# Local attention in a six-layer Trainium2 kernel: turned keys stored block-diagonally, one score matmul for two heads, all scores of a step in one PSUM bank

## The reference, cut to what matters

```python
q = l2norm(q) * qs;  k = l2norm(k) * ksc            # then rotated by position
bk2, bv2 = look(bk), look(bv)                        # each window sees the one before it and itself
sim = jnp.einsum('bhwie,bhwje->bhwij', bq, bk2) * QK_SCALE
sim = jnp.where(mask, -jnp.finfo(sim.dtype).max, sim)
attn = jax.nn.softmax(sim, -1)                       # over 64 keys
out = jnp.einsum('bhwij,bhwje->bhwie', attn, bv2)
```

## Time and profile before

| quantity | value |
|---|---|
| median of three runs | 4539.4 us (4538.72 to 4546.72) |
| profiled execution | 4539.03 us |
| its span | 4537.2 us |
| mean granted TensorE clock | 0.962 |
| TensorE busy | 4247.6 us (94%) |
| VectorE busy | 3486.7 us (77%) |
| GpSimd busy | 2585.0 us (57%) |
| ScalarE busy | 2474.6 us (55%) |
| score matmuls, L1063 | 382.4 us busy, 24576 records, mean 219 ns |
| probabilities times values, L1090 | 425.3 us busy, 10752 records, mean 280 ns |
| mask, maximum, centring (L1148, L1152, L1158) | 268.7 + 265.5 + 290.2 us busy |
| copy of the turned keys, L1204 | 227.7 us busy, 384 of 593 ns |

### The profile page before, as it was taken

How to read it: one execution, slowest core, us unless ns; L and a number is a source line. 1 busy time by engine, 2 the same in 40 slices (tenths; PEclk the granted TensorE clock), 3 DMA queues, 4 the chain that set the end, 5 groups by cost and what they waited for, 6 DMA issues and landing times. The chain is left out here.

```text
span 4537.2 us, 151497 instructions
## 1 busy us (share of the span) xinstructions
PE 4247.6 (94%) x60907; PEld 2648.5 (58%) x60907; DVE 3486.7 (77%) x6001; ACT 2474.6 (55%) x5618; POOL 2585.0 (57%) x2727
## 2 busy tenths in 40 slices
PE   6999969799998999989999989999899998999998
PEld 5999848555553555544555535555355554455553
DVE  4776556599993899966999749999479996599984
ACT  4555521466663566644666536666356664366662
POOL 2222213477771777744777617777167775277770
PEclk9999989899998999989999999999899998999998
DMA  1000000000000000000000000000000000000001
GB/s 67 0 0 0 0 0 0 6 1 0 0 0 19 6 0 0 0 19 6 0 0 0 19 5 1 0 0 0 19 6 0 0 0 19 6 0 0 0 0 38
DMA packets 12332, 27.20 MB, mean 6 GB/s; under 512 B 2460, under 2 KB 6728, under 8 KB 11344
## 3 DMA queue, kind: packets, MB, share of 16 engines
q1 hardware_dynamic: 12240, 25.80, 1.6%
HBM read 23.69 MB, written 2.10 MB: 6 GB/s over the span
## 5 line engine op out<-in xcount | busy, mean ns | idle before, releaser
L954 POOL TENSOR_TENSOR w_t<-w_t 128x512 f32<-128x512 f32 x768 | 980.9, 1278 | 352.0 <-DVE w_t L1113 349.8
L1113 DVE TENSOR_TENSOR w_t<-banks,w_tab 128x512 f32<-128x512 f32 x1536 | 982.6, 682 | 32.4 <-PE banks L1023 10.8
L983 POOL TENSOR_TENSOR w_t<-w_t,w_rn 128x512 f32<-128x512 f32 x768 | 784.4, 1042 | 243.7 <-ACT w_rn L1217 243.7
L1010 PE MATMUL banks<-w_vo,w_xs 128*32 128x256 f32 x12288 | 823.6, 386 | 8.1 <-ACT w_us L1178 8.1
L1023 PE MATMUL banks<-w_qk,w_xs 128*128 128x512 f32 x1536 | 768.9, 623 | 0.0
L1010 PEld LDWEIGHTS banks<-w_vo,w_xs 128*32 128x32 f32 x12288 | 320.9, 109 | 501.9 <-issue 357.8
L1187 ACT ACTIVATE w_pr<-w_pr 128x512 f32<-128x512 f32 x384 | 241.9, 630 | 598.8 <-DVE w_pr L1158 598.8
L1178 ACT ACTIVATE w_us<-banks 128x512 f32<-128x512 f32 x768 | 457.4, 596 | 172.4 <-PE banks L1010 172.3
L1140 DVE TENSOR_REDUCE w_ss<-w_sq 128x16 f32<-128x1024 f32 x384 | 465.2, 1211 | 0.0
L1090 PE MATMUL banks<-w_us,w_prT 128*32 128x128 f32 x10752 | 425.3, 280 | 18.5 <-ACT w_prT L1211 5.9
L975 POOL TENSOR_TENSOR w_pr<-w_pr,w_rl 128x512 f32<-128x512 f32 x384 | 403.1, 1050 | 46.1 <-DVE w_rl L1128 46.1
(11 more groups left out here) (163 smaller groups left out, 6862.4 us busy)
## 6 DMA issues: line engine op xcount, KB each, us to landing
w_qk<-w_qk_in SPq DMA_DIRECT2D x7, 1024.0 KB, 4.8
w_v<-w_v_in SPq DMA_DIRECT2D x7, 512.0 KB, 5.6
w_o<-w_o_in SPq DMA_DIRECT2D x7, 512.0 KB, 6.4
m_w<-m_w_in SPq DMA_DIRECT2D x6, 342.0 KB
xT<-x_in SPq DMA_DIRECT2D x4, 512.0 KB
out<-kept SPq DMA_DIRECT2D x8, 256.0 KB, 2.4
m_w<-m_w_in SPq DMA_DIRECT2D x6, 171.0 KB
r_tab<-r_tab_in SPq DMA_DIRECT2D x1, 512.0 KB
```

Source lines behind the costliest of these rows:

```text
L954: nc.gpsimd.tensor_tensor(v1, v1, v2[:, :, ::-1, :], ALU.add).then_inc(S["added"], 1)
L983: nc.gpsimd.tensor_tensor(v1, v1, rn[j % 2][:, i * HALF:(i + 1) * HALF].unsqueeze(2) .broadcast_to([P, HALF, WD]), ALU.mult).then_inc(S["n ...
L1010: last = nc.tensor.matmul(banks[WIN * g:WIN * (g + 1), 2, lo:lo + 2 * P], x[:, WIN * w:WIN * (w + 1)], wvo[:, first:first + 2, :].rearrang ...
L1113: nc.vector.tensor_tensor(dst[j % 2][:, i * C:(i + 1) * C].rearrange("p (h d) -> p h d", d=WD), src, tab[:, 2 * t + cs, i * WD:(i + 1) * W ...
```

## The change

- `kT` gets a dimension of two and lives for the whole program (`w_kT`, 128 partitions x 8 pairs x 2 x 288). In slot `par` only the 64 partitions of that parity hold keys; the other 64 stay zero. VectorE sets the whole tile to zero once, in the first block of the program (4608 elements a partition). The zeroing by GpSimd in each layer, with its semaphore, is gone.
- The copy of the turned keys is two copies of 64 partitions, one for each slot. Both count `k_turned`, so TensorE waits for twice the count.
- The scores of a step are 16 matmuls with 128 rows, 32 columns of queries and 128 columns of keys: both slots, each with its two windows. Since the rows of the other head are zeros, one matmul gives the scores of two heads. All 512 columns of a step go to bank 5, in the order window half, parity, group, key.
- Mask and maximum read bank 5. The centring is one instruction of 512 elements, in the place of two of 256, so `centred` counts once a step.

The diff, cut to its core:

```diff
@@ program
+    w_kT = sb("w_kT", [P, WH // 2, 2, WIN + T])
...
+            nc.vector.memset(w_kT[:], 0.0)
@@ window_attention
-    kT = sb("w_kT", [P, WH // 2, WIN + T])
...
         def _(pool):
-            nc.gpsimd.memset(kT[:, :, 0:WIN], 0.0).then_inc(S["ready"], 1)
-            pool.wait_ge(S["ready"], passed(layer + 1))
-            pool.sem_inc(sem("gate"), 1)
...
                 if live(1):
                     pe.wait_ge(S["q_turned"], passed(n(1)))
-                    pe.wait_ge(S["k_turned"], passed(n(1)))
+                    pe.wait_ge(S["k_turned"], passed(n(1) * 2))
                     if live(2):
-                        pe.wait_ge(S["centred"], passed(n(2) * 2))
+                        pe.wait_ge(S["centred"], passed(n(2)))
                     pe.sem_inc(sem("gate"), 1)
                     tk, hk = j1 // 2, j1 % 2
-                    for par in range(2):
-                        rows = slice(64 * par, 64 * par + 64)
-                        bank = banks[:, 5 + par, 0:2 * P].rearrange("p (a g r) -> p g a r", a=2, r=WIN)
-                        for g in range(NPAIR):
-                            for w in range(NWIN):
-                                lo = tk * P + WIN * w
-                                last = nc.tensor.matmul(
-                                    bank[WIN * w:WIN * (w + 1), g],
-                                    qT[j1 % 2][rows, g, WIN * w:WIN * (w + 1)],
-                                    kT[rows, hk * NPAIR + g, lo:lo + 2 * WIN].rearrange("p (a r) -> p a r", r=WIN),
-                                    start=True, stop=True)
+                    score = banks[:, 5, :].rearrange("p (a b g r) -> p g a b r", a=2, b=2, r=WIN)
+                    for g in range(NPAIR):
+                        for w in range(NWIN):
+                            lo = tk * P + WIN * w
+                            keys = kT[:, hk * NPAIR + g, :, lo:lo + 2 * WIN].rearrange("p b (a r) -> p a b r", r=WIN)
+                            last = nc.tensor.matmul(score[WIN * w:WIN * (w + 1), g],
+                                                    qT[j1 % 2][:, g, WIN * w:WIN * (w + 1)], keys,
+                                                    start=True, stop=True)
                     last.then_inc(S["scored"], 1)
...
-                    for par in range(2):
-                        nc.vector.tensor_tensor(
-                            pr[j1 % 2][:, :, par * NPAIR:(par + 1) * NPAIR].rearrange("p a g r -> p g a r"),
-                            heads[:, par], mx[j1 % 2][:, par * NPAIR:(par + 1) * NPAIR].unsqueeze(2).unsqueeze(3)
-                            .broadcast_to([P, NPAIR, 2, WIN]), ALU.subtract).then_inc(S["centred"], 1)
+                    nc.vector.tensor_tensor(pr[j1 % 2][:], heads, mx[j1 % 2][:].unsqueeze(1).unsqueeze(3)
+                                            .broadcast_to([P, 2, HALF, WIN]), ALU.subtract).then_inc(S["centred"], 1)
...
-                    nc.scalar.activation(kT[:, hk * NPAIR:(hk + 1) * NPAIR, lo:lo + P],
-                                         banks[:, 4, :].rearrange("p (g k) -> p g k", k=P), ACT.Copy)\
-                        .then_inc(S["k_turned"], 1)
+                    for par in range(2):
+                        rows = slice(64 * par, 64 * par + 64)
+                        nc.scalar.activation(kT[rows, hk * NPAIR:(hk + 1) * NPAIR, par, lo:lo + P],
+                                             banks[rows, 4, :].rearrange("p (g k) -> p g k", k=P), ACT.Copy)\
+                            .then_inc(S["k_turned"], 1)
```

More of the change, by code:

```diff
@@ L61 @@
 w_centred w_exped w_totalled w_inverse w_weighted w_p_turned w_p_taken w_valued w_y_taken w_y_turned w_residual
-w_ready w_tabled
+w_tabled
 m_up m_gelued m_made m_down m_residual
@@ L864, in window_attention @@
 @scoped
-def window_attention(nc, sem, sb, layer, h, xT, spare0, spare1, banks, ident, wqk, wv, wo, base, scl, tab, mask,
+def window_attention(nc, sem, sb, layer, h, xT, spare0, spare1, banks, ident, wqk, wv, wo, base, scl, tab, mask, kT,
                      m_w1, m_w2, m_col):
@@ L891, in window_attention @@
         "guarded logged rnorm added normed turned q_turned k_turned u_made u_taken edged scored masked maxed centred "
-        "exped totalled inverse weighted p_turned p_taken valued y_taken y_turned residual ready tabled").split()}
+        "exped totalled inverse weighted p_turned p_taken valued y_taken y_turned residual tabled").split()}
     C = HALF * WD
@@ L1184, in iteration @@
                 if live(2):
-                    act.wait_ge(S["centred"], passed(n(2) * 2))
+                    act.wait_ge(S["centred"], passed(n(2)))
                     p = pr[j2 % 2][:].rearrange("p a h r -> p (a h r)")
```

12 lines of the change are left out of this document (6 added, 6 removed).

## The result

The changed kernel takes 4571.67 us (median of four runs, 4564.28 to 4575.9); the kernel before takes 4540.41 us beside it (4538.72 to 4546.72). The ratio is 1.0065, with an interval of 1.0047 to 1.0082: 0.65% slower, where I had forecast no change, and above my range. The profiled execution took 4575.9 us, its span 4574.1. Of rival A nothing came true.

A forecast was written before the change was run, and what follows sets the result against it. Two chains of almost equal length bound it: TensorE's own instructions, and one through VectorE and GpSimd. Iterations 0 to 3 gave +0.08, -0.05, -0.01, -0.02, sum 0.00 us a turn, times 90: 4539 us, no change; range 4520 to 4566.

The forecast's parts named there:

- rival A: Faster: TensorE's drain goes, VectorE doesn't bind, the register instruction hides; 0.15 to 0.20 us a turn, 4524 us; chance 0.25.
- ScalarE's term: Second copy of the turned keys, 0.49 us start to start, hidden in ScalarE's idle time; cost 0.00 to 0.01 us.
- rival C: Slower: ScalarE's second copy at 0.60 us delays all four iterations by 0.1 us; 36 us, 4575 us; chance 0.09.
- Late scores and VectorE: Last score lands 0.09 us later, centring saves 0.07; VectorE is ready 3.18 us after the scores' start.
- rival B: Slower: scores land 0.14 us late, centring saves nothing, VectorE becomes the bound; 0.28 us a turn, 4564 us; chance 0.16.
- the centring: On VectorE, one instruction of 512 elements for two of 256 was to save 0.07 us (bounds 0 and 0.16).
- slack of 0.04: In iteration 3 VectorE was taken as ready 3.16 us after the scores' start, while the keys' rotation started at 3.20.
- The register instruction: In iteration 0, a register instruction lands ahead of the matmul on the turned probabilities: +0.08 us (bounds 0 and 0.16).
- The shorter queue: Half as many score instructions queued on TensorE let the next matmul's weights load earlier: -0.05 us in iteration 1.
- drain: On TensorE, changing tiling mode between scores and next matmul would cost a drain that now goes; rival A's gain, all four iterations.

The follow-up runs named there:

- b_full: The kernel before, with a second copy of the keys, also of all 128 partitions, into a spare tile, the scores waiting for both: 4540.31 us, ratio 1.0003.
- b_split: The kernel before, with only the one copy of the turned keys made as two copies of 64 partitions: 4561.2 us, ratio 1.0044.
- a_full: The changed kernel, with both copies of the turned keys made of all 128 partitions, so the scores mix two heads: 4544.36 us, ratio 1.0026.
- a_nomask: The changed kernel without the mask's addition to the scores, a small instruction of eight columns in its place: 4562.5 us, ratio 1.0050.
- a_twocentre: The changed kernel with the centring in two instructions of 256 elements again: 4561.47 us, ratio 1.0047.
- a_counts: The changed kernel with the single centring counting two, so iteration 0's register instruction stands ahead of the scores as before: 4565.6 us, ratio 1.0059.
- a_scale_counts: The changed kernel with a centring count of two and 128-partition copies multiplied by a column of ones and zeros, result right: 4559.59 us, ratio 1.0048.
- a_full_counts: The changed kernel with both key copies of all 128 partitions, mixing heads, and the centring counting two: 4561.98 us, ratio 1.0047.

## Why the prediction was wrong

**The step that failed is ScalarE's term.** I took 0.49 us from start to start for the new copy, from a row of 128 partitions, with 0.60 as the far end, and called it hidden at a cost of 0.00 to 0.01. Measured: 0.60 behind the first and 0.62 behind the second; both copies lose the overlap, the old one too, once it is halved. That takes 1.22 us from the first copy to the values copy where the trace before had room for 0.97. The cover that I named, 0.38 of idle time in the tightest iteration, would have held 0.48 + 0.49 (b_full: no cost) and does not hold 0.60 + 0.62 (b_split: +20 us; a_full, which takes them out of the changed kernel: 20 of its 31 us). Of the two bounds I named, the far one was the right one, and I put it in rival C at a chance of 0.09 because the shape nearest in size was not the nearest in partitions. I also changed just one of the two copies in thought.

**Rival C** had the cause and the size (4575 forecast, 4571.67 measured) but not the places. It had 0.1 in all four iterations from ScalarE; of that came 0.10 in iteration 2, and in iteration 1 the 0.05 that I expected to gain. In iteration 3 TensorE's spare 0.1 took ScalarE's delay up. In iteration 0 VectorE, which holds these scores back by 0.1, mostly covered it: a_nomask, where VectorE doesn't, has 7.93. Nor did C's 0.1 in all four follow from its rows: with 0.54 of idle time and 0.10 of overlap, one copy of 0.60 would have been hidden in iteration 0. The rest of its sum is two other causes that happened to be as large, so its 4575 is part luck.

**Late scores and VectorE** (rival B's mechanism). The term of the sum was mis-sized: the mask starts 1.15 behind the scores where I said 1.12, +0.12 instead of +0.09. And the centring saves 0.00 instead of 0.07 in iteration 3. The distance of 0.67 was read where no loop ends; at the loop's end the rotation starts 0.71 behind the first centring, whether there is one or two of them (before, after, a_twocentre). The trace shows what stands between: VectorE's sequencer takes the loop's branch and works out its registers there and in no other iteration, 90 times in the launch. The row of the branch in the changed kernel, with the shortest, median and longest duration in ns:

```profile
L905 DVEq COMPARE_BRANCH  x90: 50/56/67, 939.1 to 4450.8; - x90
```

In each of the three kernels the last register instruction ends 0.05 ahead of the rotation. I had the row before me, 2304.63 to 2305.34 in the earlier trace rows, and took its 0.04 for waiting on TensorE. So the slack of 0.04 that most of the answer hung on did not exist there: before the change VectorE and TensorE were ready within 0.01 us of each other in iteration 3. B's count of +0.10 for it is what came, +0.11.

**The register instruction** in iteration 0 was right: the rule that I read from ScalarE's rows gave +0.08, L1084's distance grew by 0.10 to 0.38 us (0.36 expected). a_counts, which puts it back ahead of the scores, has 0.28 again.

**The shorter queue** (-0.05 in iteration 1) was there but hidden: with ScalarE on time (a_full) iteration 1 is 0.08 shorter than before and L1084's first weight load comes 0.82 behind the scores in iteration 2 (0.92 before). In the changed kernel L1084 follows the turned probabilities by 0.21, 0.12 and 0.11 in iterations 1, 2 and 3, where I had 0.17 to 0.20.

**The rules of the Trainium skill.** On the drain that the Trainium skill, "TensorEngine Tiling (Array Packing)", section Key Properties, gives for a change of tiling mode, and that rival A stood beside: in a_full, where ScalarE is on time, the projection behind the scores starts 0.09 and 0.05 us earlier than before in iterations 1 and 2, which the shorter queue explains as well. These runs leave room for a drain of 0.05 us a step and don't show one. On ScalarE, the Trainium skill, "ScalarE: Activation LUTs", section What ACT_TABLE_LOAD costs, says of tiles of 128 partitions that back-to-back ACTIVATEs overlap by about 93 ns, and that each pointer operand adds as much. For 128 partitions the runs agree roughly (603 ns long and 0.49 us apart, an overlap of some 110 ns; 695 ns with the column in a_scale_counts). After 64 partitions, of which the page says nothing, there is no overlap: 587 ns long, 0.60 to 0.62 us apart.

The sum by measured terms, a turn: split copies +0.22 (b_split), new scores +0.03 (a_twocentre less b_split), single centring with the instruction that it moves +0.10 (after less a_twocentre): 0.35, times 90 is 31 us. The steps between depend on the order in which they are taken, as the waits overlap. Taken from the other end, the split copies are again 0.22 (after less a_full: 0.06, 0.08, 0.09 and 0.00 in iterations 0 to 3), and a_full's own distance from before is 0.13.

## What to carry to other kernels

Price an instruction by a row with the same number of partitions, or test it alone: half the partitions is not half the time, and here it was more than the whole. Where two instructions replace one, ask what becomes of the first, too. A slack read in one iteration of an unrolled loop doesn't hold at its end, and 0.04 us is no slack when the two ends of an unknown cost lie 0.1 apart. The number that a semaphore counts to is part of a change: it moved instructions on two engines here. When work is moved to an engine with spare time, count to the end of the queue that waits for it.

## What the runs showed of the hardware

- ScalarE, 512 columns from PSUM: the next instruction starts 0.48 to 0.50 us after one of 128 partitions, 0.57 after one with a column as its factor, 0.60 to 0.62 after one of 64 partitions, though that one itself takes no longer (587 ns mean against 603 in a_full).
- TensorE: 32 records of 128 columns in four column strips take 1.09 us busy, 64 of 64 columns in eight tiles 1.00; the mask, which reads the results, starts 0.12 later behind the first.
- A register instruction between a wait and the matmul behind it cost 0.10 us. VectorE's wait for the maximum in an instruction of its own, ahead of the centring, cost 0.06 us.
- VectorE, at the end of a loop body: 0.71 us from the centring's start to the next instruction's, for one instruction of 512 elements and for two of 256 alike. In the middle of the body it is 0.61 after the one (a_full, iteration 2).
- TensorE's clock: what lies before each layer's first scores and after its last took 1646 us with the clock at its lower level (1.2 GHz) for 293 us (a_full), and 1673 us with 381 us (a_full_counts).
- VectorE's memset of 4608 columns of float32 took 3.90 us.
